# Gated delta-rule attention and routed experts: a new order of the turn, the key convolution in the queries' buffer, accumulator pairs assigned piece by piece

## The chip, the cores and the metric

The kernel runs on one core of a Trainium2 chip. The metric is the device time of one execution in microseconds (us). The engines of the core are TensorE (PE, with its weight loads as PEld), VectorE (DVE), ScalarE (ACT), GpSimd (POOL) and SyncE (SP), which only issues transfers. Each engine works off its own list of instructions in the order written; semaphores are the only tie between them. A difference of about 0.3% is the smallest that a measurement of this kernel can tell from none.

## What is computed

One transformer block on 4 sequences of 1024 positions with 256 channels. The part that matters here is the attention: 16 heads of width 64 with a gated delta rule, clipped.

```python
q = einsum('btd,cd->bct', h, Wq); k = ...Wk; v = ...Wv
q = silu(causal_conv(q)); k = silu(causal_conv(k)); v = silu(causal_conv(v))   # 4 taps
k = k / max(norm(k), 1e-12)
alpha = sigmoid(h @ Wa.T + ba); beta = sigmoid(h @ Wb.T + bb)
def step(S, (kt, vt, qt, at, bt)):
    v_old = S @ kt
    dS = outer(vt - at * v_old, kt)
    S = clip(at * S + bt * dS, -5, 5)
    return S, S @ qt
x = x + ga * (y * silu(h @ Wg.T + bg)) @ Wo.T
x = x + gb * moe(layernorm(x))          # 8 experts, 2 per token
```

## The kernel before, in words

The program is a chain of stages: `front` (layer norm, gates, step sizes), `delta_fast` (the whole attention recurrence), `judge`, `attn_out`, `moe`. The change is in `delta_fast` alone.

`delta_fast` works in 16 **turns** (`TURNS`), one for each pair of heads and pair of sequences. A turn does three things at once, each for another unit: `it` runs from -1 to 17; unit `u = it` is **prepared** (`prep`), unit `tc = it - 1` goes through its recurrence (`chain`), and unit `tb = it - 2` gets the bound that tells whether the clip could matter. A turn is cut into 16 slots `c`, one for each chunk of 64 positions of the chain; in each slot the chain does one link: `seed_u` and `state_into_u` (PE), `keep_u` (ACT), `state_sum` (PE), `state` (DVE, a copy for `c = 0`). Between the links stand pieces of the preparation, in an order written out by hand, `if prep and c == 5: ...`, on ACT, DVE and PE. On PE a slot has two places, ahead of `state_sum` and behind it.

The preparation of a unit, with the line of its work in brackets:

- K: `proj_k` (PE L976, 4 matrix products of 128x512 for each of the two sequences), `first_k` (ACT L530), `taps_k` (DVE L730, three passes for each sequence), `silu_k` (ACT L544).
- `kk` (PE L1012), 64x64 products of the keys with each other, two blocks `h`, each written in two halves of 32 rows in the trace.
- `decay(u, h)` (DVE L799), a scan over a row of step sizes that SP loads into the one buffer `d_al`; the load for `h = 1` waits until the scan for `h = 0` has read it. `solve_matrix(u, h)` (DVE L811, two passes), `join` (ACT L574), `turn_matrix` (DVE L819), `scalars` (DVE L828 to L834).
- `solve` (POOL L671 and L676): 31 rows of a forward substitution, in `d_TT`, two instructions each.
- meanwhile Q and V: `proj_qv(u, j, i)` for j = 0 to 3 (Q of two sequences, V of two), `first_qv`, `taps_qv`, `silu_qv`; `k_turned` (PE L1045) and `keep_k`; `kq` (PE L1012 with `d_qT`) and `attention` (DVE L857); `decayed_q` (DVE L851).
- when the solve is done: `turn_x` (DVE L872) and `rows_of_x` (DVE L879) transpose its result. `cross_first` (PE L1104) needs `rows_of_x` only; `keep_x` (ACT L588) and `cross_second` (PE L1117) need `turn_x` too, and `cross_second` needs `keep_cross_first` (ACT L595). `keep_cross` (ACT L602) ends that part. Then `v_turned` (PE L1045) and `scale_v` (DVE L866), `decayed_x` (DVE L883), `w_products` (PE L1139) and `keep_w` (ACT L616), `largest_k` (DVE L840), and K of unit u + 1, which begins the next turn.
- of the bound: `bound_terms` (POOL L687), `z_turned` (PE L1091), `bound_scan` (DVE L786), `bound_max` (DVE L793), `update_max` (DVE L768). Of the output: `y_of_state` (L1190), `y_of_u` (L1202), `turn_y` (DVE L760). POOL also decays the keys, `decay_k` (L703), which `state_sum` needs; it waits for `largest_k` and for `w_products`.

All pieces of the preparation that PE writes share four PSUM banks, as two **pairs** (`pair(at)`, banks 4 and 5, or 6 and 7). Before, a table gives each piece a place `AT_...` from 0 to 19 in a ring, and its pair is the place modulo 2. A piece may write a pair once the piece ahead of it on that pair has been read; these are the waits in `proj_k`, `proj_qv`, `kk`, `kq`, `turned` and so on. `conv_dst` says where a convolution is built: Q in `d_qT`, K in the memory of `d_TT` and `d_Tq` (`k_made`), V in that of `d_Xn`. As `d_TT` holds the solve and then the cross products, `first_k` waits for `s_x2` (`keep_cross`).

## Time and profile before

| | us |
|---|---|
| median of three runs | 2378.34 (2376.22 to 2382.27) |
| the profiled execution | 2367.01 |
| its span | 2365.4 |
| first and last `turn_matrix` (DVE L819), 15 turns apart | 105.6 and 1537.7 |
| PE, DVE, POOL, ACT busy | 81%, 63%, 42%, 32% of the span |

The profiled execution is 11.3 us shorter than the median, and 1.6 us of it lie around the span. In the profile a line like `L811 DVE TENSOR_TENSOR d_TT<-d_ps,d_D` is one instruction of VectorE written in line 811, with the tile that it writes ahead of the arrow. `[1.07 <-DMA d_al]` behind a row is the idle time of that engine just before it, and what ended it.

### The profile page before, as it was taken

What the parts mean: (1) busy time and instruction counts of PE and PEld (TensorE: products, weight loads), DVE (VectorE), ACT (ScalarE), POOL (GpSimd) and SP (SyncE); (2) the same over time, 40 slices, a digit from 0 to 9 for tenths busy, and PEclk for the clock granted to TensorE, in tenths of its full rate; (3) what the DMA queues carried; (4) which work ended last, traced back from release to release, by engine and by line L of the source; (5) the groups of instructions that cost most, each with busy time, mean ns of one, the idle gap of its engine ahead of it and who ended that gap; (6) DMA issues with size and microseconds to landing.
All of it is one profiled execution on the core that took longest, in us unless ns stands there. A gap on an engine that the chain in (4) does not pass through costs nothing. (4 is left out here: it accounts for less than half of the span.)

```text
span 2365.4 us, 59283 instructions
## 1 busy us (share of the span) xinstructions
PE 1924.9 (81%) x24750; PEld 1379.2 (58%) x24750; DVE 1489.1 (63%) x2181; ACT 760.4 (32%) x1250; POOL 1004.0 (42%) x1316
## 2 busy tenths in 40 slices
...
DMA packets 89029, 156.52 MB, mean 66 GB/s; under 512 B 15676, under 2 KB 54084, under 8 KB 87564
## 3 DMA queue, kind: packets, MB, share of 16 engines
...
## 5 line engine op out<-in xcount | busy, mean ns | idle before, releaser
L976 PE MATMUL d_ps<-hT,d_w 128*128 128x512 f32 x768 | 414.4, 659 | 16.3 <-DMA d_cw<-convp_in 11.9
L703 POOL TENSOR_TENSOR d_ktok<-d_ktok,decay_tok 128x512 f32<-128x512 f32 x64 | 95.6, 1523 | 510.0 <-DVE d_kmax L840 487.3
L676 POOL TENSOR_TENSOR d_TT<-d_TT,d_tmp 128x31 f32<-128x31 f32 (+15 forms) x496 | 284.0, 573 | 38.9
L671 POOL TENSOR_TENSOR d_tmp<-d_Tq,d_TT 128x31 f32<-128x31 f32 (+15 forms) x496 | 262.8, 530 | 73.8 <-DVE d_TT L834 36.2
L976 PEld LDWEIGHTS d_ps<-hT,d_w 128*128 128x128 f32 x768 | 138.4, 206 | 121.0 <-issue 89.7
L1157 PE MATMUL d_ps<-d_Vp,d_XTz 64*64 64x64 f32 x2048 | 143.2, 261 | 65.3 <-DVE d_S L750 64.3
L569 ACT ACTIVATE d_U<-d_ps 128x128 f32<-128x128 f32 x256 | 70.2, 274 | 383.1 <-PE d_ps L1165 379.8
L750 DVE SCALAR_TENSOR_TENSOR d_S<-d_S,gamma_chunk,d_ps 128x64 f32<-128x64 f32 x448 | 106.9, 291 | 135.2 <-PE d_ps L1174 135.1
L1157 PEld LDWEIGHTS d_ps<-d_Vp,d_XTz 64*64 64x64 f32 x2048 | 111.1, 163 | 125.0 <-issue 124.7
L2043 POOL DMA_INDIRECT out<-m_yo,m_slot_i x71 | 112.7, 1587 | 131.6 <-DVE m_yo L2143 86.2
L1784 POOL TENSOR_TENSOR y<-y,g_sb 128x512 f32<-128x512 f32 x64 | 102.5, 1632 | 124.2 <-ACT g_sb L1768 123.6
L2022 ACT ACTIVATE m_hm<-m_ps,m_b_tile 128x128 f32<-128x128 f32 x284 | 81.2, 368 | 226.8 <-PE m_ps L2191 226.8
L730 DVE SCALAR_TENSOR_TENSOR d_Xn<-d_ps,d_cw,d_Xn 128x1023 f32<-128x1023 f32 (+2 forms) x96 | 122.8, 1279 | 42.8 <-ACT d_Xn L530 41.6
L2181 PE MATMUL m_ps<-m_w,m_xs 128*128 x284 | 138.3, 610 | 8.3 <-issue 6.5
L1202 PE MATMUL d_ps<-d_U,d_A 64*64 64x64 f32 x2048 | 130.0, 249 | 6.9
L2202 PE MATMUL m_ps<-m_w,m_hm 128*128 x568 | 134.4, 380 | 0.0
L1202 PEld LDWEIGHTS d_ps<-d_U,d_A 64*64 64x64 f32 x2048 | 95.9, 151 | 61.9 <-issue 39.5
...
L1647 PE MATMUL o_pg<-h_split,wg_split 128*128 128x512 f32 x384 | 92.5, 399 | 39.3 <-DVE wo_split L1640 31.9
L730 DVE SCALAR_TENSOR_TENSOR d_qT<-d_ps,d_cw,d_qT 128x1023 f32<-128x1023 f32 (+2 forms) x96 | 121.3, 1277 | 1.2
L1012 PE MATMUL d_ps<-d_kT 64*64 64x64 f32 x2048 | 115.7, 280 | 6.8 <-ACT d_kT L544 6.8
L1647 PE MATMUL o_po<-wo_split,y_split 128*128 128x256 f32 x768 | 105.8, 305 | 16.2 <-DVE y_split L1640 16.2
...
## 6 DMA issues: line engine op xcount, KB each, us to landing
...
y_scratch<-d_yT SPq DMA_DIRECT2D x256, 64.0 KB, 2.0
d_arow<-ab_scratch SPq DMA_DIRECT2D x128, 128.0 KB, 3.0
...
```

The source lines that it names most:

```text
L671: nc.gpsimd.tensor_tensor(tv, Tq[:, s + 1:, s].rearrange("p (r a) -> p r a", a=1).broadcast_to([P, left, known]), X[:, s, 0:known].rearran ...
L676: nc.gpsimd.tensor_tensor(X[:, s + 1:, 0:known], X[:, s + 1:, 0:known], tv, ALU.subtract).then_inc(s_sub, 1)
L730: nc.vector.scalar_tensor_tensor(out=dst[:, j + 1:], in0=src[:, 0:T - 1 - j], scalar=cw[:, u // BP % 2, n, 2 - j:3 - j], in1=dst[:, j + 1: ...
L750: last = nc.vector.scalar_tensor_tensor(out=S[:, (c + 1) % SLOTS, b2, :], in0=S[:, c % SLOTS, b2, :], scalar=gC[:, b2, tc * NCW + c:tc * N ...
L976: return nc.tensor.matmul(dst[:, g, :], w[:, m % 2, n, dc, :], hT[:, dc, at:at + G], start=(dc == 0), stop=(dc == DC - 1))
L1012: last = nc.tensor.matmul(chunks(pair(at), CW)[rows64(b2), c, :], kT[rows64(h), c, b2, :], by(c, b2), start=True, stop=True)
L1157: last = nc.tensor.matmul(u_ps(c)[rows64(b2), h, :], XTz[rows64(b2), tc % 2, h * NCW + c, :], Vp[rows64(b2), c, rows64(h)], start=True, st ...
L1202: last = nc.tensor.matmul(y_ps(c, h, b2), A[rows64(b2), tc % 2, h, c, :], U[rows64(b2), c % KEPT, h, :].rearrange("p (j v) -> p j v", j=2) ...
L1647: ins = nc.tensor.matmul(dst, lhs(a).bitcast(F32R), rhs(b).bitcast(F32R), start=first and n == 0, stop=last and n == 2)
L2043: nc.gpsimd.indirect_dma_start(out, bass.IndirectOffsetOnAxis(ap=slot_i[:, j:j + 1], axis=0), yo[:, j % YRING, :], None, compute_op=ALU.ad ...
L2181: last = nc.tensor.matmul(ps[:, j % 2, :], xs[:, j % 2, dc * P:(dc + 1) * P], w1_s[:, bass.ds(e, 1), dc, :].rearrange("p a f -> p (a f)"), ...
L2202: last = nc.tensor.matmul(dst, hm[:, j % 2, f * P:(f + 1) * P], w2_s[:, bass.ds(e, 1), f, :].rearrange("p a d -> p (a d)"), start=f == 0, ...
```

## The change

The piece order of a turn is written anew on ACT, DVE and PE; POOL and SP are as before. K's convolution is built in `d_qT`, so `first_k` waits for `kq` and `decayed_q` of the unit ahead, no longer for `keep_cross`, and `first_qv` of Q waits for `silu_k`. The ring is gone; each piece has its pair, 0 or 1, by name, and each wait for a pair names the piece that is now ahead on it. Instructions and their sizes are the same. The core of the diff, one or two lines of each of the order tables:

```diff
-RING = 20
-(AT_KK0, AT_KK1, AT_Q0, AT_Q1, AT_KT0, AT_V0, AT_KT1, AT_KQ0, AT_V1, AT_Z0,
- AT_KQ1, AT_P, AT_Z1, AT_X, AT_VT0, AT_VT1, AT_K0, AT_K1, AT_WA, AT_WB) = range(RING)
+(AT_KK0, AT_Q0, AT_V0, AT_KT0, AT_Z0, AT_KQ1, AT_P, AT_X, AT_K0, AT_WA, AT_WB,) = (0,) * 11
+(AT_KK1, AT_Q1, AT_KQ0, AT_KT1, AT_V1, AT_Z1, AT_VT0, AT_VT1, AT_K1,) = (1,) * 9
...
-            return (qT[:, b2, :], k_made[b2], v_made)[n]
+            return (qT[:, b2, :], qT[:, b2, :], v_made)[n]
...
             def first_k(u, b2):
...
-                act.wait_ge(s_x2, u)
+                act.wait_ge(s_kq, 2 * u)
+                act.wait_ge(s_qg, u)
...
                 if i < 2:
-                    act.wait_ge(s_kq, 2 * u)
-                    act.wait_ge(s_qg, u)
+                    act.wait_ge(s_ksilu, 2 * u + 2)
...
                     if prep and c == 12:
                         taps_qv(u, 3, (2,))
+                        attention(u, 1)
+                        rows_of_x(u)
                         turn_x(u)
-                        rows_of_x(u)
-                    if prep and c == 13:
-                        attention(u, 1)
...
                     if b2 == 0:
                         if it >= 0:
-                            pe.wait_ge(s_V, 2 * it + 1)
+                            pe.wait_ge(s_x2, it + 1)
...
                     if h == 0:
                         if it >= 1:
-                            pe.wait_ge(s_wt, 2 * it - 1)
+                            pe.wait_ge(s_wt, 2 * it)
...
                     else:
-                        if it < TURNS - 1:
-                            pe.wait_ge(s_ktap, 6 * it + 12)
-                        else:
-                            pe.wait_ge(s_V, 2 * it + 2)
+                        pe.wait_ge(s_wt, 2 * it + 1)
```

The last piece is `w_products(u, 1)`: both W products stand on pair 0 now, so the second waits until `keep_w(u, 0)` has read the first, and `kk(u + 1, 0)` waits until `keep_w(u, 1)` has.

**Place 1, PE, the cross products (end of the solve).** L1104 (after: L1097) is `cross_first`, L1091 (L1087) `z_turned(1)`, L1157 and L1165 (L1147, L1155) the chain's `seed_u` and `state_into_u`, L1174 (L1164) `state_sum`, L1117 (L1110) `cross_second`, L1045 (L1041) `v_turned`. Before:

```order
L1104 MATMUL d_ps<-d_Xn,d_TTx 32x32 x64
L1091 MATMUL d_ps<-ident,d_Z 128x2x64 x8
L1157 MATMUL d_ps<-d_Vp,d_XTz 64x64 x4
L1165 MATMUL d_ps<-d_S,d_WT 64x64 x4
L1117 MATMUL d_ps<-d_Tq,d_TT 32x32 x32
L1174 MATMUL d_ps<-d_U,d_ktok 64x64 x4
L1117 MATMUL d_ps<-d_Tq,d_TT 32x32 x32
L1045 MATMUL d_ps<-ident,d_vT 128x128 x8
L1157 MATMUL d_ps<-d_Vp,d_XTz 64x64 x4
L1165 MATMUL d_ps<-d_S,d_WT 64x64 x4
L1045 MATMUL d_ps<-ident,d_vT 128x128 x4
```

After:

```order
L1087 MATMUL d_ps<-ident,d_Z 128x2x64 x8
L1097 MATMUL d_ps<-d_Xn,d_TTx 32x32 x32
L1147 MATMUL d_ps<-d_Vp,d_XTz 64x64 x4
L1155 MATMUL d_ps<-d_S,d_WT 64x64 x4
L1097 MATMUL d_ps<-d_Xn,d_TTx 32x32 x32
L1164 MATMUL d_ps<-d_U,d_ktok 64x64 x4
L1041 MATMUL d_ps<-ident,d_vT 128x128 x4
L1110 MATMUL d_ps<-d_Tq,d_TT 32x32 x64
L1041 MATMUL d_ps<-ident,d_vT 128x128 x4
L1147 MATMUL d_ps<-d_Vp,d_XTz 64x64 x4
L1155 MATMUL d_ps<-d_S,d_WT 64x64 x4
```

`z_turned(1)` stands ahead of `cross_first`, which is cut in two by a link of the chain, and half of the V transposes stand ahead of `cross_second`.

**Place 2, DVE, the key convolution of the next unit.** L730 (L729) are `taps_k`, L840 (L839) `largest_k`, L768 (L767) `update_max`, L748 (L747) the chain's first `state`. Before:

```order
L866 TENSOR_TENSOR d_Vp<-d_ps,d_n 128x1024
L730 SCALAR_TENSOR_TENSOR d_TT<-d_ps,d_cw,d_TT 128x1023
L730 SCALAR_TENSOR_TENSOR d_TT<-d_ps,d_cw,d_TT 128x1022
L730 SCALAR_TENSOR_TENSOR d_TT<-d_ps,d_cw,d_TT 128x1021
L730 SCALAR_TENSOR_TENSOR d_Tq<-d_ps,d_cw,d_Tq 128x1023
L730 SCALAR_TENSOR_TENSOR d_Tq<-d_ps,d_cw,d_Tq 128x1022
L730 SCALAR_TENSOR_TENSOR d_Tq<-d_ps,d_cw,d_Tq 128x1021
L840 TENSOR_REDUCE d_kmax<-d_ktok 128x128
L768 TENSOR_REDUCE d_um<-d_U 128x128
L748 COPY d_S<-d_ps 128x64 x2
L799 SCALAR_TENSOR_TENSOR d_D<-d_al,d_msk 128x1024
```

After:

```order
L865 TENSOR_TENSOR d_Vp<-d_ps,d_n 128x1024
L839 TENSOR_REDUCE d_kmax<-d_ktok 128x128
L729 SCALAR_TENSOR_TENSOR d_qT<-d_ps,d_cw,d_qT 128x1023
L729 SCALAR_TENSOR_TENSOR d_qT<-d_ps,d_cw,d_qT 128x1022
L729 SCALAR_TENSOR_TENSOR d_qT<-d_ps,d_cw,d_qT 128x1021
L729 SCALAR_TENSOR_TENSOR d_qT<-d_ps,d_cw,d_qT 128x1023
L729 SCALAR_TENSOR_TENSOR d_qT<-d_ps,d_cw,d_qT 128x1022
L729 SCALAR_TENSOR_TENSOR d_qT<-d_ps,d_cw,d_qT 128x1021
L747 COPY d_S<-d_ps 128x64 x2
```

`largest_k` is ahead of the taps and `update_max(2)` two slots earlier; the taps write `d_qT`.

**Place 3, PE and DVE, the start of the turn.** On PE, L1012 (L1008) is `kk`, L976 (L972) `proj_qv(0)`, L1190 and L1202 (L1180, L1192) the outputs. PE before:

```order
L1012 MATMUL d_ps<-d_kT 64x64 x16
L1174 MATMUL d_ps<-d_U,d_ktok 64x64 x4
L1190 MATMUL d_ps<-d_S,d_qg 64x2x32 x4
L1202 MATMUL d_ps<-d_U,d_A 64x2x32 x4
L1157 MATMUL d_ps<-d_Vp,d_XTz 64x64 x4
L1165 MATMUL d_ps<-d_S,d_WT 64x64 x4
L1012 MATMUL d_ps<-d_kT 64x64 x16
L1190 MATMUL d_ps<-d_S,d_qg 64x2x32 x4
L1174 MATMUL d_ps<-d_U,d_ktok 64x64 x4
L1202 MATMUL d_ps<-d_U,d_A 64x2x32 x4
L1012 MATMUL d_ps<-d_kT 64x64 x16
L1157 MATMUL d_ps<-d_Vp,d_XTz 64x64 x4
```

PE after:

```order
L1164 MATMUL d_ps<-d_U,d_ktok 64x64 x4
L1008 MATMUL d_ps<-d_kT 64x64 x16
L1180 MATMUL d_ps<-d_S,d_qg 64x2x32 x4
L1147 MATMUL d_ps<-d_Vp,d_XTz 64x64 x4
L1155 MATMUL d_ps<-d_S,d_WT 64x64 x4
L1008 MATMUL d_ps<-d_kT 64x64 x16
L1164 MATMUL d_ps<-d_U,d_ktok 64x64 x4
L1008 MATMUL d_ps<-d_kT 64x64 x16
L1147 MATMUL d_ps<-d_Vp,d_XTz 64x64 x4
L1155 MATMUL d_ps<-d_S,d_WT 64x64 x4
L1192 MATMUL d_ps<-d_U,d_A 64x2x32 x4
L1164 MATMUL d_ps<-d_U,d_ktok 64x64 x4
```

The first `state_sum` is ahead of `kk`, one `kk` block is left for the slot behind, and no projection is ahead of the third `state_sum` (the last row here); before, `proj_qv(0)` stands there, two rows below the piece shown. On DVE, L799 (L798) is `decay`, L811 (L810) `solve_matrix`, L760 (L759) `turn_y`, L750 (L749) `state`. DVE before:

```order
L799 SCALAR_TENSOR_TENSOR d_D<-d_al,d_msk 128x1024
L750 SCALAR_TENSOR_TENSOR d_S<-d_S,gamma_chunk,d_ps 128x64 x2
L811 TENSOR_TENSOR d_TT<-d_ps,d_D 128x512
L811 TENSOR_TENSOR d_TTx<-d_ps,d_D 128x512
L760 STREAM_TRANSPOSE d_yT<-d_ps 128x512 x2
L750 SCALAR_TENSOR_TENSOR d_S<-d_S,gamma_chunk,d_ps 128x64 x2
L799 SCALAR_TENSOR_TENSOR d_D<-d_al,d_msk 128x1024
L811 TENSOR_TENSOR d_TT<-d_ps,d_D 128x512
L811 TENSOR_TENSOR d_TTx<-d_ps,d_D 128x512
```

DVE after:

```order
L798 SCALAR_TENSOR_TENSOR d_D<-d_al,d_msk 128x1024
L767 TENSOR_REDUCE d_um<-d_U 128x128
L749 SCALAR_TENSOR_TENSOR d_S<-d_S,gamma_chunk,d_ps 128x64 x2
L810 TENSOR_TENSOR d_TT<-d_ps,d_D 128x512
L810 TENSOR_TENSOR d_TTx<-d_ps,d_D 128x512
L749 SCALAR_TENSOR_TENSOR d_S<-d_S,gamma_chunk,d_ps 128x64 x2
L759 STREAM_TRANSPOSE d_yT<-d_ps 128x512 x2
L798 SCALAR_TENSOR_TENSOR d_D<-d_al,d_msk 128x1024
L810 TENSOR_TENSOR d_TT<-d_ps,d_D 128x512
L810 TENSOR_TENSOR d_TTx<-d_ps,d_D 128x512
```

`turn_y` stands behind the third `state` (the second L749 here), just ahead of the second `decay`, and `update_max(3)` has gone from ahead of `turn_matrix` to behind the first `decay`.

## Rows read from the trace of the kernel before

**Rows 1.** The page: each engine's busy time, share of the span, instructions.
```profile
PE 1924.9 (81%) x24750; PEld 1379.2 (58%) x24750; DVE 1489.1 (63%) x2181; ACT 760.4 (32%) x1250; POOL 1004.0 (42%) x1316
```

**Rows 2.** One line of the kernel, `turn_matrix`: count, durations, first and last start.
```profile
L819 DVE STREAM_TRANSPOSE d_Tq<-d_TT x16: 1917/1956/1989, 105.6 to 1537.7; 128x1024 f32<-128x1024 f32 x16
```

**Rows 3.** DVE in order of time: start, duration, operation [idle before, releaser]; four stations.
```profile
815.82 1.93 DVE L872 STREAM_TRANSPOSE d_Tq<-d_TT 128x1024 f32<-128x1024 f32 x1 [5.73 <-POOL d_TT L676]
...
867.81 1.94 DVE L819 STREAM_TRANSPOSE d_Tq<-d_TT 128x1024 f32<-128x1024 f32 x1 [1.17 <-ACT d_TT L574]
...
911.86 1.95 DVE L872 STREAM_TRANSPOSE d_Tq<-d_TT 128x1024 f32<-128x1024 f32 x1 [3.27 <-POOL d_TT L676]
...
961.61 1.95 DVE L819 STREAM_TRANSPOSE d_Tq<-d_TT 128x1024 f32<-128x1024 f32 x1 [1.21 <-ACT d_TT L574]
```

**Rows 4.** POOL in order of time: end of one solve, start of the next.
```profile
911.78 1.92 POOL L687 TENSOR_TENSOR d_Z<-d_um,d_kmax 128x1024 f32<-128x1024 f32 x1
...
966.66 0.25 POOL L671 TENSOR_TENSOR d_tmp<-d_Tq,d_TT 128x31 f32<-128x31 f32 x1 [2.09 <-DVE d_TT L834]
```

**Rows 5.** Groups of instructions by line: busy, mean ns | idle before, releaser; `silu_k(1)`, `keep_w`.
```profile
L616 ACT ACTIVATE d_WT<-d_ps 128x1024 f32<-128x1024 f32 x32 | 32.8, 1024 | 21.8 <-PE d_ps L1139 21.8
...
L544 ACT ACTIVATE d_kT<-d_Tq 128x1024 f32<-128x1024 f32 x16 | 16.9, 1057 | 20.6 <-DVE d_Tq L730 20.6
```

**Rows 6.** PE in order of time, behind the solve that ended at 815.8.
```profile
819.76 3.49 PE L1104 MATMUL d_ps<-d_Xn,d_TTx 32*32 32x32 f32 x123
823.18 1.97 PE L1091 MATMUL d_ps<-ident,d_Z 128*128 128x128 f32 x8
...
826.28 1.92 PE L1117 MATMUL d_ps<-d_Tq,d_TT 32*32 32x32 f32 x64
```

**Rows 7.** ACT in order of time, the same turn: `keep_cross`, `first_k`.
```profile
830.51 2.04 ACT L602 ACTIVATE d_XTz<-d_ps 32x1024 f32<-32x1024 f32 x2 [3.81 <-PE d_ps L1117]
838.82 1.20 ACT L530 ACTIVATE d_TT<-d_ps,d_cw 128x1024 f32<-128x1024 f32 x1 [6.27 <-PE d_ps L976]
```

**Rows 8.** DVE in order of time, the same turn, from `scale_v` to `solve_matrix`.
```profile
837.12 1.23 DVE L866 TENSOR_TENSOR d_Vp<-d_ps,d_n 128x1024 f32<-128x1024 f32 x1 [1.14 <-PE d_ps L1045]
840.06 3.92 DVE L730 SCALAR_TENSOR_TENSOR d_TT<-d_ps,d_cw,d_TT 128x1023 f32<-128x1023 f32 x3 [1.71 <-ACT d_TT L530]
843.89 3.91 DVE L730 SCALAR_TENSOR_TENSOR d_Tq<-d_ps,d_cw,d_Tq 128x1023 f32<-128x1023 f32 x3
847.71 2.28 DVE L840 TENSOR_REDUCE d_kmax<-d_ktok 128x128 f32<-128x2048 f32 x1
...
852.01 2.28 DVE L799 TENSOR_TENSOR_SCAN d_D<-d_al,d_msk 128x1024 f32<-128x1024 f32 x1
...
861.96 2.28 DVE L799 TENSOR_TENSOR_SCAN d_D<-d_al,d_msk 128x1024 f32<-128x1024 f32 x1
...
864.94 0.68 DVE L811 TENSOR_TENSOR d_TTx<-d_ps,d_D 128x512 f32<-128x512 f32 x1
```

**Rows 9.** PE in order of time, the same turn's start: `kk`, `proj_qv`.
```profile
849.52 1.91 PE L1012 MATMUL d_ps<-d_kT 64*64 64x64 f32 x30
...
859.00 2.07 PE L976 MATMUL d_ps<-hT,d_w 128*128 128x512 f32 x2
```

**Rows 10.** Stretches: us, busy by engine (PE, PEld, DVE, ACT, POOL), granted clock, DMA share, GB/s.
```profile
848.70:862.20 13.50, 13.30 (x243) 11.04 (x236) 7.96 (x14) 2.05 (x5) 7.97 (x5) 0.50 0.46 118
...
931.00:944.00 13.00, 10.15 (x138) 5.53 (x140) 10.26 (x9) 5.00 (x6) 0.00 (x0) 1.00 0.01 1
944.30:947.60 3.30, 3.30 (x99) 3.30 (x91) 2.10 (x2) 1.71 (x3) 1.71 (x2) 0.50 0.03 7
947.70:962.00 14.30, 12.96 (x269) 8.87 (x265) 11.57 (x18) 3.22 (x6) 6.16 (x4) 1.00 0.62 155
```

**Rows 11.** DVE in order of time, the next turn: last tap of K, second `decay`.
```profile
939.71 3.91 DVE L730 SCALAR_TENSOR_TENSOR d_Tq<-d_ps,d_cw,d_Tq 128x1023 f32<-128x1023 f32 x3
...
955.75 2.29 DVE L799 TENSOR_TENSOR_SCAN d_D<-d_al,d_msk 128x1024 f32<-128x1024 f32 x1 [1.07 <-DMA d_al<-steps_scratch]
```

264 lines of the change are left out of this document (130 added, 134 removed).

## The prediction

> **What bounds the kernel now.** The page comes first, and it misleads: PE is busy for 81% of the span [rows 1], so one looks for fewer or faster products. The view of single lines corrects this. `turn_matrix` runs once a turn, and 15 turns lie between its first start at 105.6 and its last at 1537.7 [rows 2]: 1432.1 / 15 = 95.47 us a turn. What decides those 95.47 us is a ring, read off DVE in order of time [rows 3]. From `turn_matrix` at 867.81 to `turn_x` at 911.86 are 44.05 us, and DVE stood idle for 3.27 us ahead of `turn_x` (5.73 in the turn ahead), each time for POOL. This is the **solve half**: POOL starts at 966.66, 5.05 after `turn_matrix` at 961.61, and is done at 911.78, right when `turn_x` starts [rows 3, 4]. PE's load there costs nothing as long as DVE is ready before POOL.
>
> The other part, from `turn_x` to the next `turn_matrix`, is the **K half**: the cross products, the convolution of the next keys, `kk`, `solve_matrix`, `join`. It took 51.99 us from 815.82 to 867.81 and 49.75 from 911.86 to 961.61 [rows 3]. The mean is 95.47 - 44.05 = 51.42, so about (51.99 - 51.42) / (51.99 - 49.75) = one turn in four is of the short kind. What parts the two kinds is TensorE's clock at the start of the turn [rows 10]: granted 0.50 (1.2 GHz) for all of 848.7 to 862.2 in the long one; in the short one 0.50 only from 944.3 to 947.6, then 1.00 (2.4 GHz). Both falls follow a time in which PE waits for K's taps (PE is busy for 10.15 of the 13.0 us ahead of 944.3). In the short turn W products and `kk` then filled the stretch without a gap (3.30 busy of 3.30), and the clock rose; in the long one it rose only after a large product, `proj_qv`, had run at 859.00 [rows 9].
>
> **The change, part by part.** Nothing is added or removed, so every term is a move. Times below are counted from `turn_x`'s place x = 815.82 in the long turn.
>
> (1) *Solve half.* `attention(1)` (1.2 us) comes ahead of the transposes and has to fit into DVE's idle time of 3.27 to 5.73 us [rows 3]. The V convolution of the first sequence starts earlier. `turn_y` moves within the half. POOL's list is unchanged. Price: 0, hidden behind POOL; if the cover failed, each us of lateness of DVE would be 15 us in all.
>
> (2) *Cross products.* Before, `cross_first` ends at 819.76 + 3.49 = x+7.4, `cross_second` starts at 826.28 and `keep_cross` ends at 830.51 + 2.04 = x+16.7 [rows 6, 7]. After, `rows_of_x` comes first, which would free `cross_first` 2 us earlier. But on PE `z_turned(1)` is now ahead of it, and waits for POOL's `bound_terms` of 1.92, which starts when the solve ends [rows 4]. So: 1.9, `z_turned` 1.9 to x+3.8 [rows 6], half of `cross_first` 1.8, a link of the chain 1.2 (from the end of `z_turned` at 825.15 to 826.28 it took 1.13), the other half 1.8: x+8.6. `keep_cross_first`, which I price like `keep_cross` at 2.04, x+10.7. `cross_second` as one piece 2 x 1.92 = 3.84 [rows 6], x+14.5. `keep_cross` x+16.6. Net -0.1: the 2 us are spent on the transposes of Z.
>
> (3) *Taps of K.* The K projection needs `keep_cross` (pair 0), x+16.6. Half of the V transposes lie behind it, interleaved with the projections. A 128x512 product takes 2.07 at the low clock [rows 9], about half at the high one. With the clock rising as now around x+19 the second V transposes are out at x+20.7, `scale_v(1)` 1.23 and `largest_k` 2.28 [rows 8] follow: x+24.2. `first_k` is done at x+23.8, so `largest_k` is what the taps wait for. They start at x+24.2, before at 840.06, also x+24.2. They end at T = x+32.0 as before. Net 0; bounds -0.4 (the short turn's start) and +1.4 (the clock rises one K product later, at the low price).
>
> (4) *From the taps to the first `decay`.* Before: 843.89 + 3.91 = T = 847.80 to 852.01, 4.2 us, with `largest_k` 2.28 in it [rows 8]. After, the path runs over ACT: `silu_k(1)` 1.06, `keep_w(1)` 1.02 [rows 5], then `keep_u(0)`, `state_sum` and `state`, for which I take 1.2, what a link of the chain took in (2): the first `decay` at T+3.3. The new wait is here: with both W products on pair 0, `kk(0)` and `keep_u(0)` are queued behind `keep_w(1)`, and `kk` starts at T+2.9, where it started at about T+1.6 (849.52 is its third row [rows 9]). I get a gain of 0.9 on DVE and a loss of 1.3 on PE.
>
> (5) *From there to the end of `solve_matrix`.* Before, at the low clock: 864.94 + 0.68 = T+17.8 [rows 8]. After, at the low clock: `kk` blocks of 1.8 each, at T+2.9, T+6.2 and T+8.2, links of 1.0 to 1.5 between them, the third `state` at T+12.2 because neither a projection of 2.07 nor a fourth `kk` block stands ahead of it. `turn_y` 1.3, then the second `decay` from T+13.8 to T+16.1. The last `kk` block stands behind `proj_qv(0)` and a link, to about T+16.2; two passes of 0.68 give T+17.5. Net -0.3. At the high clock I get T+14.5. Before, with T = 939.71 + 3.91 = 943.62, the second `decay` at 955.75 waits for its transfer [rows 11]; 2.29 of its own and 1.4 for the two passes (864.24 to 865.62 in the long turn [rows 8]) give T+15.8. Net -1.3.
>
> *Sum.* A long turn: 51.99 - 0.3 = 51.69. A short one: 49.75 - 1.3 + 0.2 for (4)'s later start = 48.65. The sum hangs on how many turns are short. PE now stands still three times ahead of `kk`: from the end of the K projections to the end of the first taps, about 2 us, as the outputs that filled this time have moved two slots ahead; between the two W products, 1 us for `keep_w(0)`; and 2.3 us from the last W product to `state_sum(0)`. The short turn's clock rose out of W products and `kk` without a gap; that sequence no longer occurs. I take no short turns: 51.69 - 51.42 = +0.27 a turn, 15 x 0.27 = **+4 us**. Against the profiled execution 2367.0 + 4 = 2371; the median of the runs is 11.3 above it and I keep that distance: 2378.3 + 4 = **2382**.
>
> The Trainium skill, page "TensorE: Matmul & The Clock Gate", section "Why this matters for your kernels", says that gaps of idle time between bursts of products bring the clock back down, and that TensorE is to be kept busy. The trace agrees on the fall at 944.3 [rows 10]; on the long turn's stretch, busy for 13.30 of 13.50 us at 0.50, busy time alone did not bring it back. By the page's rule a `kk` stretch that is busy throughout would regain the clock soon, and every turn would be short.
>
> **Rivals.** *The clock comes back early.* The mechanism is the one of the short turn: `kk`, the links and the outputs now run with three blocks close together, and if that is enough the turns take 48.65: 15 x (48.65 - 51.42) = -42, 2337. If only today's share of one in four stays short: 0.25 x 48.65 + 0.75 x 51.69 = 50.93, 15 x -0.49 = -7, 2371. For it: 3.30 of 3.30 busy raised the clock once [rows 10]. Against it: 13.30 of 13.50 did not.
>
> *Slower: the clock rises later behind the cross products.* Half of the V transposes, 128 wide, now stand far ahead of the K projection, so the stretch that raised the clock is thinner. If the first two K products and the last V transposes run at 1.2 GHz, `largest_k` and the taps start 0.8 to 1.4 us later. With the +0.27 this is 15 x 1.1 to 15 x 1.7 = +16 to +25: 2394 to 2403. It decides against the kernel from a delay of 0.2 us a turn on, since 15 x 0.47 is 7.
>
> *The moves do not do what they say* in the solve half: DVE is late for the transposes, as `bound_max(0)` now holds `kq(1)`, which `attention(1)` waits for. The 3.27 to 5.73 us of idle time less 1.2 leave 2.1 to 4.5, so this needs a large error; 1 us of lateness gives +15, 2397.
>
> **How the numbers follow.** The forecast case, no short turns and the terms right to within 0.45 us a turn, has 0.42; all of it lies within 0.3% (7.1 us, about what a measurement of this kernel can tell from no change). The early clock, in whole or for a share of the turns, has 0.27, from 2337 to 2371. The late clock has 0.26, a late DVE 0.05: together 0.31 on the slow side. The range leaves out the last part of the early clock (0.1) and the end of the late one (0.1): 2350 to 2398; the forecast case alone is 2375 to 2386.
>
> **What would show it.** Right: the solve half stays 44.05; DVE's idle ahead of `rows_of_x` is several us and for POOL; `cross_first` starts 3.8 to 3.9 behind `rows_of_x`, as now; the taps of K start at x+24 right behind `largest_k`; the first `decay` starts 3.3 behind the end of the taps; the K half is 51.4 to 52.0 in nearly every turn; the granted clock is 0.50 across `kk` in all turns. Wrong: K halves of 49 or less in many turns (the early clock); taps later than x+24.8 (the late clock); a `rows_of_x` that follows `attention(1)` without idle time (DVE late).

## The result and the profile after

| | before | after |
|---|---|---|
| median of 8 runs beside each other, us | 2377.08 (2366.23 to 2382.27) | 2361.80 (2358.32 to 2365.61) |
| ratio, 95% interval | | 0.9946 [0.9931, 0.9961] |
| once more, beside each other, median | 2373.69 of 29 runs | 2365.27 of 10 runs, 0.9966 [0.9951, 0.9981] |
| the profiled execution, and its span | 2367.01, 2365.4 | 2365.61, 2364.0 |

By the two ratios the change makes the kernel faster by 0.3% to 0.5%. I forecast 2382, a little slower and no measurable difference. The time lies in my range, but the direction and the likeliest case were wrong.

The two profiled executions differ by only 1.4 us and mislead: before's lay low among its runs, after's high. I therefore profiled both kernels a second time (`before_again`, `after_again`). The page and one line of the kernel, `turn_matrix`, which answer to [rows 1, 2]:

```profile
PE 1902.9 (80%) x24750; PEld 1356.3 (57%) x24750; DVE 1499.0 (63%) x2181; ACT 756.1 (32%) x1250; POOL 980.7 (41%) x1316
```

```profile
L818 DVE STREAM_TRANSPOSE d_Tq<-d_TT x16: 1925/1946/1960, 105.1 to 1535.3; 128x1024 f32<-128x1024 f32 x16
```

15 turns take 1430.2 us (before: 1432.1), in the second execution 1424.7 (before: 1435.6).

**A long turn of after.** DVE in order of time, from the first transpose at x = 1006.05 to the next `turn_matrix` (start, duration, operation; it answers to [rows 3, 8]):

```profile
1006.05 2.05 DVE L878 STREAM_TRANSPOSE d_Xn<-d_TT 128x1024 f32<-128x1024 f32 x1 [6.64 <-POOL d_TT L675]
...
1028.43 2.28 DVE L839 TENSOR_REDUCE d_kmax<-d_ktok 128x128 f32<-128x2048 f32 x1
1030.62 7.73 DVE L729 SCALAR_TENSOR_TENSOR d_qT<-d_ps,d_cw,d_qT 128x1023 f32<-128x1023 f32 x6
...
1041.65 3.81 DVE L798 TENSOR_TENSOR_SCAN d_D<-d_al,d_msk 128x1024 f32<-128x1024 f32 x1
...
1051.27 2.25 DVE L798 TENSOR_TENSOR_SCAN d_D<-d_al,d_msk 128x1024 f32<-128x1024 f32 x1
...
1054.60 0.68 DVE L810 TENSOR_TENSOR d_TTx<-d_ps,d_D 128x512 f32<-128x512 f32 x1
...
1057.46 1.95 DVE L818 STREAM_TRANSPOSE d_Tq<-d_TT 128x1024 f32<-128x1024 f32 x1 [1.80 <-ACT d_TT L572]
```

The solve half is as before, bounded by POOL with 6.64 us of idle time on DVE. The K half is 51.41: taps at x+24.6, first `decay` at x+35.6, 3.3 behind the end of the taps, end of `solve_matrix` at x+49.2. From 910.47 on the turns repeat to within 0.06 us (95.54 to 95.60). PE and ACT behind the same x (they answer to [rows 6, 7]):

```profile
1007.95 1.97 PE L1087 MATMUL d_ps<-ident,d_Z 128*128 128x128 f32 x8 [8.02 <-POOL d_Z L686]
1009.85 1.92 PE L1097 MATMUL d_ps<-d_Xn,d_TTx 32*32 32x32 f32 x64
...
1012.89 1.92 PE L1097 MATMUL d_ps<-d_Xn,d_TTx 32*32 32x32 f32 x64
...
1017.04 3.63 PE L1110 MATMUL d_ps<-d_Tq,d_TT 32*32 32x32 f32 x128 [0.77 <-ACT d_TT L593]
```

```profile
1020.71 2.04 ACT L600 ACTIVATE d_XTz<-d_ps 32x1024 f32<-32x1024 f32 x2 [3.81 <-PE d_ps L1110]
```

`rows_of_x` is out of the way 2 us earlier, and `z_turned(1)` (L1087) spends it: `keep_cross` (L600) starts at x+14.7 as before. The clock, in stretches from x+35.5 to x+48.0 of five turns (columns as in [rows 10], the granted clock is the third number from the end):

```profile
375.30:387.80 12.50, 12.02 (x249) 8.10 (x244) 10.21 (x17) 2.42 (x5) 4.12 (x2) 1.00 0.64 150
...
661.60:674.10 12.50, 12.00 (x257) 8.21 (x251) 10.36 (x17) 2.20 (x5) 4.34 (x2) 1.00 0.62 155
754.50:767.00 12.50, 12.31 (x214) 10.00 (x212) 10.21 (x13) 0.83 (x3) 2.04 (x2) 0.52 0.43 113
...
1041.50:1054.00 12.50, 12.31 (x215) 9.94 (x211) 10.08 (x14) 0.83 (x3) 1.81 (x1) 0.53 0.44 112
1137.10:1149.60 12.50, 12.31 (x214) 9.94 (x210) 10.09 (x14) 0.83 (x3) 1.79 (x1) 0.53 0.44 115
```

In the turns of 339.79 and 626.11 the clock stays at 2.4 GHz and their K halves are 48.56 and 48.76; in the other turns from the fourth on the stretch is at 0.50 to 0.54, nearly all of it 1.2 GHz, and the K halves are 51.4 to 52.2. The first two turns are neither kind (49.63 and 50.16) and are taken up below.

**Where the time went.** From the DVE rows of all 15 turns of both executions of each kernel, K halves in us:

| | before | after |
|---|---|---|
| turns 4 to 15: mean | 51.37 | 51.35 |
| of these under 50.3 (short) | 8 of 24, mean 49.77 | 2 of 24, mean 48.87 |
| the others (long) | 52.17 | 51.57 |
| turns 1 to 3: mean (lowest, highest) | 51.15 (48.08, 52.79) | 48.86 (47.38, 50.16) |
| solve half, mean of all turns | 44.26 | 44.32 |
| last `turn_matrix` to the first cast of the next stage | 152.6, 152.4 | 149.5, 149.3 |

The steady turns gained nothing. The first three gained 3 x (51.15 - 48.86) = 6.9 us, the drain behind the last turn 3.1, and 0.8 went back in the solve halves (15 x 0.05): about -9.5 (-0.3, -6.9, +0.8, -3.1), against -8.1 and -12.8 by the two ratios. The -6.9 is a mean of two executions that lie apart: the first three K halves sum to 152.0 and 154.9 in before, to 148.3 and 144.8 in after. Two kernels from below, which measured like before and like after, agree with it: 153.8 in `before_max_ahead`, 148.0 in `after_k_in_tt`. From the cast on, the stages behind run the same instructions, but took 675.1 and 682.5 in the two executions of before and 679.2 and 682.0 in those of after: the first page of before owes 7 us to that.

### The profile page after: what moved, and what is told of

It reads as the page before. It is cut to its first block and busy times, and to the rows that moved or that the text cites. A ratio compares the mean times of both kernels' runs of the same rounds, so it can differ in the third digit from the quotient of the medians.

```text
span 2364.0 us, 59315 instructions
## 1 busy us (share of the span) xinstructions
PE 1902.9 (80%) x24750; PEld 1356.3 (57%) x24750; DVE 1499.0 (63%) x2181; ACT 756.1 (32%) x1250; POOL 980.7 (41%) x1316
## 3 DMA queue, kind: packets, MB, share of 16 engines
q1 hardware_dynamic: 72860, 124.76, 17.5%
## 5 line engine op out<-in xcount | busy, mean ns | idle before, releaser
L972 PE MATMUL d_ps<-hT,d_w 128*128 128x512 f32 x768 | 429.0, 676 | 28.1 <-DVE d_qT L729 12.8
L670 POOL TENSOR_TENSOR d_tmp<-d_Tq,d_TT 128x31 f32<-128x31 f32 (+15 forms) x496 | 279.1, 563 | 75.2 <-DVE d_TT L833 37.6
L675 POOL TENSOR_TENSOR d_TT<-d_TT,d_tmp 128x31 f32<-128x31 f32 (+15 forms) x496 | 269.5, 543 | 38.9
L702 POOL TENSOR_TENSOR d_ktok<-d_ktok,decay_tok 128x512 f32<-128x512 f32 x64 | 66.5, 1060 | 463.8 <-PE d_ps L1129 442.9
L729 DVE SCALAR_TENSOR_TENSOR d_qT<-d_ps,d_cw,d_qT 128x1023 f32<-128x1023 f32 (+2 forms) x192 | 242.8, 1277 | 21.1 <-ACT d_qT L528 17.7
L972 PEld LDWEIGHTS d_ps<-hT,d_w 128*128 128x128 f32 x768 | 139.1, 209 | 125.3 <-issue 81.2
L749 DVE SCALAR_TENSOR_TENSOR d_S<-d_S,gamma_chunk,d_ps 128x64 f32<-128x64 f32 x448 | 109.3, 302 | 88.1 <-PE d_ps L1164 84.0
L1147 PEld LDWEIGHTS d_ps<-d_Vp,d_XTz 64*64 64x64 f32 x2048 | 113.4, 163 | 85.6 <-issue 84.3
L1147 PE MATMUL d_ps<-d_Vp,d_XTz 64*64 64x64 f32 x2048 | 145.5, 261 | 16.7 <-DVE d_S L749 14.4
L729 DVE SCALAR_TENSOR_TENSOR d_Xn<-d_ps,d_cw,d_Xn 128x1023 f32<-128x1023 f32 (+2 forms) x96 | 122.2, 1273 | 43.7 <-ACT d_Xn L528 42.5
L1087 PE MATMUL d_ps<-ident,d_Z 128*128 128x128 f32 x256 | 50.7, 363 | 113.9 <-POOL d_Z L686 113.9
L1192 PE MATMUL d_ps<-d_U,d_A 64*64 64x64 f32 x2048 | 132.7, 249 | 7.8
L528 ACT ACTIVATE d_qT<-d_ps,d_cw 128x1024 f32<-128x1024 f32 x64 | 77.1, 1205 | 175.6 <-issue 96.9
L694 POOL MEMSET d_TT<- 128x1024 f32 x16 | 15.2, 952 | 283.3 <-DVE d_Tq L818 283.3
L1192 PEld LDWEIGHTS d_ps<-d_U,d_A 64*64 64x64 f32 x2048 | 100.4, 152 | 50.7 <-issue 25.0
```

The costliest lines, as they stand in the source:

```text
L670: nc.gpsimd.tensor_tensor(tv, Tq[:, s + 1:, s].rearrange("p (r a) -> p r a", a=1).broadcast_to([P, left, known]), X[:, s, 0:known].rearran ...
L675: nc.gpsimd.tensor_tensor(X[:, s + 1:, 0:known], X[:, s + 1:, 0:known], tv, ALU.subtract).then_inc(s_sub, 1)
L729: nc.vector.scalar_tensor_tensor(out=dst[:, j + 1:], in0=src[:, 0:T - 1 - j], scalar=cw[:, u // BP % 2, n, 2 - j:3 - j], in1=dst[:, j + 1: ...
L749: last = nc.vector.scalar_tensor_tensor(out=S[:, (c + 1) % SLOTS, b2, :], in0=S[:, c % SLOTS, b2, :], scalar=gC[:, b2, tc * NCW + c:tc * N ...
L972: return nc.tensor.matmul(dst[:, g, :], w[:, m % 2, n, dc, :], hT[:, dc, at:at + G], start=(dc == 0), stop=(dc == DC - 1))
L1147: last = nc.tensor.matmul(u_ps(c)[rows64(b2), h, :], XTz[rows64(b2), tc % 2, h * NCW + c, :], Vp[rows64(b2), c, rows64(h)], start=True, st ...
```

## The experiments

Fifteen-turn times below run from the first start of `turn_matrix` to the last, in one profiled execution; before is 1432.1 and 1435.6, after 1430.2 and 1424.7.

### The same two kernels again, and the transposes swapped alone

`before_again` is before, `after_again` is after, unchanged.

> The kernel before, unchanged, to see how far one execution of it differs from the next. Theory 'mix': its executions differ in how many of the 15 K halves (from turn_x or rows_of_x to the next turn_matrix) are short (under 50.5 us, clock back at 2.4 GHz within the kk stretch) or long (52 us); the profiled one of the prediction held more short ones than is usual, so this one has a sum of 15 turns (first to last start of turn_matrix) above 1432, up to 1441, and a span that follows it. Rival 'elsewhere': the 15 turns take 1432 again within 2 us, and what differs between executions lies in the stages behind the recurrence. Ratio to before 1.000.

> The changed kernel, unchanged, beside before on one chip. Theory 'mix': ratio about 0.994 to 0.996; in the profile most K halves are 51.4 us, the sum of 15 turns is 1425 to 1432, so the distance to the sum of before_again is 5 to 12 us. Rival 'elsewhere': the sums of 15 turns of the two differ by under 3 us, and the last unit's recurrence and what follows it carry the rest.

Ratios 1.0006 [0.9992, 1.0019] and 0.9966 [0.9951, 0.9981]. The gain is there again, a little smaller; two executions of one kernel differ by up to 5.5 us in the fifteen turns. Both of my cases for before hold in part: its two spans differ by 11.8 us, of which 3.6 lie in the turns and 7.4 in the stages behind.

`before_rows_first` makes one of the change's moves in before:

```diff
                     if prep and c == 12:
                         taps_qv(u, 3, (2,))
-                        turn_x(u)
                         rows_of_x(u)
+                        turn_x(u)
```

> The kernel before with rows_of_x ahead of turn_x on VectorE, nothing else. cross_first needs rows_of_x only. Theory 'the ring is bound link by link': cross_first starts 2.05 behind the first transpose in place of 3.8, cross_second at 8.7 in place of 10.5, and each K half is 1.7 shorter: 15 x 1.7 = 25 us, ratio 0.989. Rival 'the K half is held elsewhere' (by the V transposes, bound_max or the K projection): under 8 us, ratio 0.997 or more.

2366.31, ratio 0.9948 [0.9921, 0.9975], fifteen turns 1428.5. `cross_first` starts at x+2.10 instead of x+3.83, `keep_cross` ends at x+15.0 instead of x+16.7, the taps start at x+22.9 in the mean instead of x+24.1, and the K half is 50.52 in the mean, 0.8 less than before's 51.33. Solve halves of 45.3 in several turns give some of it back. The time lies between my two cases, at half of the 25 us. This one swap is worth as much as the whole change, though its twelve runs spread widely: four lie from 2342.5 to 2354.3, eight from 2363.8 to 2372.9, and the profiled one (2367.15) is of the eight. Its first three K halves sum to 146.8: the swap alone takes as much from them as the change does. In before the head of the K half can be shortened, and in the steady turns the change spends that on `z_turned(1)`.

### After, with the cross products in before's order

```diff
                     if prep and c == 13:
                         cross_first(u, 0)
+                        cross_first(u, 1)
+                    if tb >= 0 and c == 13:
+                        z_turned(it, 1)
                     if prep and c == 14:
-                        v_turned(u, 0, 0)
-                        cross_second(u, 0)
                         cross_second(u, 1)
+                        v_turned(u, 0, 0)
                         v_turned(u, 0, 1)
```

(`z_turned(1)` is taken from ahead of `cross_first`, `cross_second(0)` stands where `cross_first(1)` was, and `keep_cross_first` goes one slot ahead on ACT.)

> The changed kernel with the cross products in the order of before on TensorE (cross_first whole, then z_turned(1), cross_second in two halves, V transposes behind them) and keep_cross_first right behind keep_x on ScalarE; rows_of_x stays ahead of turn_x. Theory 'z_turned(1) ahead of cross_first spends what rows_of_x first would give': cross_first starts at 2.05 in place of 3.8, cross_second at 8.7 in place of 11.0, the K half is 1.5 to 2 us shorter than in after: ratio to before 0.983 to 0.986. Rival: the taps start when they do now, at 24.6, as scale_v(1) and largest_k hold them: ratio 0.994.

2341.01 (2334.33 to 2346.43), ratio 0.9868 [0.9846, 0.9891], close to the 0.983 to 0.986 of my theory: 1.3% in place of the change's 0.3% to 0.5%, faster than both kernels. DVE and PE of one turn, x = 1086.09:

```profile
1086.09 2.05 DVE L878 STREAM_TRANSPOSE d_Xn<-d_TT 128x1024 f32<-128x1024 f32 x1 [6.44 <-POOL d_TT L675]
...
1107.79 2.27 DVE L839 TENSOR_REDUCE d_kmax<-d_ktok 128x128 f32<-128x2048 f32 x1
```

```profile
1088.19 3.63 PE L1097 MATMUL d_ps<-d_Xn,d_TTx 32*32 32x32 f32 x128 [8.02 <-DVE d_Xn L878]
1091.75 1.97 PE L1087 MATMUL d_ps<-ident,d_Z 128*128 128x128 f32 x8
1094.85 1.92 PE L1110 MATMUL d_ps<-d_Tq,d_TT 32*32 32x32 f32 x64
1097.12 1.92 PE L1110 MATMUL d_ps<-d_Tq,d_TT 32*32 32x32 f32 x64
```

`cross_first` starts at x+2.1, and `z_turned(1)` falls into the time in which PE waits for ACT's copy. From the third turn on `keep_cross` ends at x+15.0 and the taps start at x+22.5 to x+24.0; K halves are 47.7 to 50.9, fifteen turns 1407.8. The order of the change in this place costs about 20 us (1427.5, the mean of after, less 1407.8; by the medians 2365.27 less 2341.01, 24 us). The run moves three things together: `z_turned(1)`, the cut of `cross_first` by a link, and `keep_cross_first` on ACT. What each is worth by itself was not measured.

### Single parts of the change taken back

`after_wb_pair1`: the second W product on pair 1, as in before, with the waits that belong to it.

```diff
-(... AT_K0, AT_WA, AT_WB,) = (0,) * 11
-(... AT_VT1, AT_K1,) = (1,) * 9
+(... AT_K0, AT_WA,) = (0,) * 10
+(... AT_VT1, AT_K1, AT_WB,) = (1,) * 10
...
-                        pe.wait_ge(s_wt, 2 * it + 1)
+                        if it < TURNS - 1:
+                            pe.wait_ge(s_ktap, 6 * it + 12)
```

> The changed kernel with the second W product on pair 1 in place of pair 0, so that it waits for the last tap of K as before, kk(0) only for the first keep_w and kk(1) for the second. Theory 'the pair of W': the W product moves behind the taps, keep_w(1) and the chain's keep_u(0) behind it follow 1.0 to 1.5 us later, the first decay starts at T+4.5 in place of T+3.3 (T is the end of K's taps), and the K half grows by 1: +15 us, ratio near 1.001. Rival 'W and kk without a gap bring the clock back early': more K halves under 50.5, the K half no longer, ratio 0.990 to 0.996.

2381.65, ratio 1.0037 [1.0022, 1.0051], fifteen turns 1442.8. They grow by 15 us as in my theory; the ratio is above its 1.001. The first `decay` starts 4.7 behind the end of the taps (T) in the mean, with pair 0 it was 3.2. On pair 1 the product waits for the last tap of K; on pair 0 it only waits for a copy on ACT. The pair is worth about 15 us of the fifteen turns.

`after_k_in_tt`: K's convolution in the memory of `d_TT` and `d_Tq`, with before's waits.

```diff
-            return (qT[:, b2, :], qT[:, b2, :], v_made)[n]
+            return (qT[:, b2, :], k_made[b2], v_made)[n]
```

> The changed kernel with K's convolution built in the memory of TT and Tq as before, with the waits of before for it (first_k on keep_cross, Q's first_qv on kq and decayed_q). Both theories: no change, since the K projection, on pair 0, waits for keep_cross in any case; ratio 0.994 to 0.997, all stations of the K half within 0.1 us. If the queries' memory matters the taps start later than 24.6 and the kernel is over 5 us slower than after.

2366.09, ratio 0.9962 [0.9948, 0.9977], as after: the memory of the convolution has no effect.

`after_largest_behind`: `largest_k` behind the taps, as before.

```diff
                         scale_v(u, 1)
-                        largest_k(u)
...
                         taps_k(u + 1, 1, (2,))
+                    if prep and c == 15:
+                        largest_k(u)
```

> The changed kernel with largest_k behind the taps of K, as before. The taps may then start when first_k is done, 0.4 us earlier at most (24.2). Theory 'largest_k holds the chain': GpSimd's decay_k waits for largest_k, 2.28 behind the taps, and takes 1 to 1.5 us, state_sum(0) waits for it, so the first decay moves from T+3.3 to about T+4.5; net +0.8 a turn, +12 us, ratio near 1.000. Rival 'it is hidden': ScalarE's two silu and keep steps of 3.3 us cover it, the turn gains 0.4, ratio 0.991 to 0.994.

2362.02 (2348.16 to 2371.78), ratio 0.9946 [0.9925, 0.9968], as after; neither of my cases (near 1.000, or 0.991 to 0.994) came. The profiled execution is the slowest of its eight, with fifteen turns of 1435.8. In it the taps start 0.4 earlier in the mean and the first `decay` comes at T+4.1 instead of T+3.2, so at that point it is 0.5 behind. The times show no such loss; what makes up for it was not found.

`after_qv_ahead`: the first projection of Q ahead of the third `state_sum`, as before.

```diff
+                    if prep and c == 2:
+                        proj_qv(u, 0, 0)
                     if prep and c == 3:
                         kk(u, 1, 1)
```

(It goes from behind `state_sum(2)` to ahead of it.)

> The changed kernel with one product put back: proj_qv(0,0) stands ahead of the third state_sum on TensorE, as before. Theory 'start of the turn': where the kk stretch runs at 1.2 GHz this product takes 2.07 us ahead of state_sum(2), which the third state and with it the second decay and solve_matrix wait for, so the long K half grows from 51.5 by 1 to 2 us and the kernel by 10 to 25 us (ratio to before 1.000 to 1.006). Rival 'the gain lies in the cross products or at the taps': no change, ratio 0.994 to 0.997.

2371.34, ratio 0.9985 [0.9973, 0.9998]. Long K halves grow to 52.7 to 53.4, the second `decay` comes at x+47.0 instead of x+45.2, as the third `state` waits for the projection. In this profile every second turn is short, so that its fifteen turns (1429.8) are hardly longer than after's. Why they are short there is not known. The move of this projection is a gain of some 0.2% to 0.4%.

`before_max_ahead`: `update_max(3)` in slot 0 in before, to test one explanation of the shorter drain.

```diff
+                    if tb >= 0 and c == 0:
+                        update_max(tb, 3)
...
-                    if tb >= 0 and c == 2:
-                        update_max(tb, 3)
```

> Before, with update_max(3) on DVE moved from slot 2 to slot 0, as the change does: the one move held responsible for 2.6 us of the 3.1 us by which the drain behind the last turn became shorter. Theory: from the last turn_matrix to the first cast of the next stage 150.0 instead of 152.6; the turns get no shorter (it now stands between decay and solve_matrix, in idle time): ratio 0.998 to 1.000. Rival: the drain is shortened by the new order as a whole and not by this move: 152.5, ratio 1.000; or the move delays solve_matrix by its own length each turn, ratio over 1.002.

2376.75, ratio 1.0001 [0.9992, 1.0011], the drain is 152.5: my explanation fell. PE at the end of the chain in this kernel, and in after:

```profile
1664.76 0.49 PE L1165 MATMUL d_ps<-d_S,d_WT 64*64 64x64 f32 x8
...
1671.04 1.97 PE L1091 MATMUL d_ps<-ident,d_Z 128*128 128x128 f32 x8
```

```profile
1657.05 0.49 PE L1155 MATMUL d_ps<-d_S,d_WT 64*64 64x64 f32 x8
...
1661.17 1.97 PE L1087 MATMUL d_ps<-ident,d_Z 128*128 128x128 f32 x8
```

From the last link's product to the transposes of Z behind the outputs are 6.28 us in before and in this kernel, 4.12 in after: the outputs of five chunks stand between them there, of three here. These 2.2 us are most of the 3.1. It is read from the traces; no run took it away alone.

### Does TensorE's clock part long from short turns?

`after_filler`, `cross_filler` and `before_filler` add matrix products of 128x320 that nobody reads, into PE's idle time in the K half (the expectations of after and before call them 128x128; they were 320 columns wide). In after:

```diff
+            def filler(tc, n):
+                ...
+                for _ in range(n):
+                    nc.tensor.matmul(ps[:, 0, 3 * DH:], ident[:], hT[:, 0, 0:G - 3 * DH], start=True, stop=True)
...
                     if prep and c == 15:
+                        filler(tc, 5)
                         w_products(u, 0, 0)
                         w_products(u, 0, 1)
+                        filler(tc, 2)
                         w_products(u, 1, 0)
...
+                        filler(tc, 3)
```

> After, with idle time of PE in the K half filled by matrix products 128x128 whose result nobody reads (it adds work and leaves nothing out): 5 ahead of the first W product (PE waits for the first taps of K there), 2 between the two W products, 3 behind the last W product. Theory: what parts long from short turns is TensorE's clock while kk runs; with large products in the gaps it is 1.00 there in nearly all turns, the K half is 47.4 to 50.2 in nearly all (51.4 in 11 of 15 now), the next solve half 45.4 to 45.8 instead of 44.1; per turn 0.6 to 1.5 less, 9 to 22 us in all: ratio to before 0.985 to 0.991. Rival: the clock of kk is a companion and not the cause, or the products don't hold it up; then they are mere work on PE's list, K halves stay at 51.4 or get longer by up to 1: ratio 0.995 to 1.001.

> The kernel after with the cross products in the order of before (2341.0), with the same added products as in the kernel above. Its K halves were 47.7 to 50.85 without them. Theory (clock of kk decides): where its turns already run kk at the high clock there is nothing left to win there; I expect K halves of 47.7 to 49 and a ratio of 0.984 to 0.988. Rival (added products are only work): K halves longer by 0.5 to 1, ratio 0.990 to 0.993.

> Before, with 4 products 128x128 that nobody reads between the two W products, where PE waits for the second taps of K. Theory: kk runs at 1.00, the K half is 49.6 to 50.0 in nearly all turns (short kind of before) instead of one in three to four: 15 x 1.5 = 22 us at most, ratio 0.990 to 0.994. Rival: no effect of the clock: ratio 1.000 to 1.004.

After with them: 2372.20, ratio 0.9985 [0.9975, 0.9995]; the fast kernel of the section above: 2349.99, 0.9885 [0.9867, 0.9903]; before: 2379.01, 1.0008 [0.9989, 1.0027]. After, the added products and the clock behind x = 815.00, and DVE:

```profile
843.27 2.96 PE L1140 MATMUL d_ps<-hT,ident 128*128 128x320 f32 x10 [1.51 <-ACT d_U L567]
...
850.01 1.88 PE L1140 MATMUL d_ps<-hT,ident 128*128 128x320 f32 x6
```

```profile
850.50:863.00 12.50, 11.65 (x260) 8.56 (x258) 8.92 (x13) 1.53 (x5) 3.40 (x3) 1.00 0.41 113
```

```profile
853.43 2.61 DVE L798 TENSOR_TENSOR_SCAN d_D<-d_al,d_msk 128x1024 f32<-128x1024 f32 x1
...
863.81 0.68 DVE L810 TENSOR_TENSOR d_TTx<-d_ps,d_D 128x512 f32<-128x512 f32 x1
```

The clock is held at 1.00, and from the first `decay` to the end of `solve_matrix` are 11.1 us instead of 13.6. But 6.2 us of added work, of which 2.96 could only start when ACT had read the same bank, moved the first `decay` from x+35.6 to x+38.4. In the sum nothing is gained: after loses 0.2% to 0.4% by it, and the fast kernel's ratio lies between my two cases. In before the added products let nine K halves be short instead of four or five. In the turn of 816.10 they held the clock some four us longer, then it fell all the same (0.68 in 853.00:854.00, 0.50 behind that); five of the six K halves that stayed long rose to 53.3 to 53.7.

`after_lean_filler` and `cross_lean_filler` add less (5 and 2 products of 128x192 and 2 of 128x128), in a bank that ACT does not read then:

```diff
                     if prep and c == 15:
+                        filler(5, 5)
                         w_products(u, 0, 0)
                         w_products(u, 0, 1)
+                        filler(2, 5)
                         w_products(u, 1, 0)
...
+                        filler(2, 6)
```

> After, with smaller added products that nobody reads, sized to fit into PE's idle time: 5 of 128x192 ahead of the first W product, 2 between the W products, 2 of 128x128 behind the outputs that end the turn; they write a part of PSUM that ACT does not read at that time, so that they need not wait for keep_u(15). In the kernel with 128x320 products the granted clock was 1.00 all through kk and the first decay came to the end of solve_matrix in 10.9 us instead of 13.6, but the added products themselves ended late and moved the first decay from T+3.3 to T+5.65. Theory (the clock of kk parts long turns from short ones): first decay at T+2.7 to T+3.5, solve_matrix 10.9 later, K halves of 48.4 to 49.2 in nearly all turns, given back 1.5 in the next solve half; 15 x about 1 less than after: ratio to before 0.987 to 0.991. Rival (the gain was an artefact of the later start, the work before kk having piled up): K halves stay at 51.4, ratio 0.994 to 0.997.

> The kernel after with the cross products of before, and the same smaller added products. In its run without them the K halves were 47.7 to 50.85, so some turns lost the clock in kk. Theory: all turns at the high clock, K halves 47 to 48.5, ratio 0.981 to 0.986 (without: 0.9868). Rival: nothing gained, 0.986 to 0.990.

After: 2360.83, ratio 0.9940 [0.9922, 0.9959], fifteen turns 1418.6 in an execution that is the fastest of its six. The fast kernel: 2335.34 (2327.82 to 2338.95), ratio 0.9817 [0.9783, 0.9852], fifteen turns 1396.9. Four turns of after with the lean products, from x+35.5 to x+48.0; their K halves are, in this order, 50.8, 49.2, 50.6 and 49.2:

```profile
466.70:479.20 12.50, 10.73 (x204) 8.20 (x201) 10.34 (x13) 0.83 (x3) 1.52 (x1) 0.69 0.54 131
562.40:574.90 12.50, 11.14 (x210) 7.51 (x207) 10.84 (x15) 1.84 (x4) 0.92 (x1) 0.86 0.59 148
...
1037.10:1049.60 12.50, 10.70 (x196) 7.95 (x192) 10.34 (x13) 0.83 (x3) 1.28 (x1) 0.68 0.53 141
...
1323.70:1336.20 12.50, 11.28 (x209) 7.53 (x205) 10.70 (x15) 1.78 (x4) 0.75 (x1) 0.86 0.55 148
```

And the fast kernel with them, K halves 50.00, 47.24, 48.12 and 47.56:

```profile
460.90:473.40 12.50, 10.72 (x177) 7.65 (x174) 10.62 (x15) 1.04 (x4) 0.80 (x1) 0.67 0.59 149
555.90:568.40 12.50, 10.44 (x187) 6.47 (x176) 9.62 (x16) 3.39 (x6) 0.00 (x0) 1.00 0.69 182
647.50:660.00 12.50, 10.50 (x193) 6.68 (x188) 9.67 (x15) 2.56 (x4) 0.00 (x0) 1.00 0.67 168
739.80:752.30 12.50, 10.34 (x188) 6.45 (x185) 9.39 (x16) 3.09 (x6) 0.00 (x0) 1.00 0.75 182
```

The end of the K half follows the clock: from the first `decay` to the end of `solve_matrix` are 13.6 us at 0.53 (after), 13.2 at 0.69 and 11.7 at 0.86 (the first two turns above). The first `decay` starts at T+3.0 to T+3.1 in them, no later than in after, so the rival of a gain by a later start falls. Adding work that nobody needs shortens the K half: the mean of turns 4 to 15 of after falls from 51.35 to 50.24. From the third turn on the stretches of after stood at 0.64 to 0.86, and in the fast kernel only some were at 1.00, so my size of it (all turns at 48.4 to 49.2) was too large. On the times the lean products in after can't be told from none (0.9940 and 0.9946, 0.9966); in the fast kernel the ratio falls from 0.9868 to 0.9817, with intervals that overlap a little, from five and four runs. The best version is `cross_lean_filler`, 1.8% faster than before. What holds the clock in one turn and not in the next stays open.

## Why the prediction was wrong, point by point

- **The solve half and (1): right.** 44.05 taken, 44.0 to 44.2 measured in most turns; DVE waits 6.64 us for POOL. Some are longer because POOL starts later: in after five are 44.7 to 45.8, with POOL's first row 5.6 to 6.7 behind `turn_matrix` instead of 5.05, and each stands directly ahead of a short K half (45.79 ahead of 48.76, for one). A short turn is thus worth less than its K half says. Why the two go together I did not follow up. In before, too, the mean is 44.23 and not 44.05, so my 51.42 for its mean K half should have been 51.24, and 5 of its 15 K halves were short, not one in four.
- **(2), right.** Forecast x+8.6, x+14.5, x+16.6 for the ends of `cross_first`, `cross_second`, `keep_cross`; measured x+8.8, x+14.6, x+16.7. The run with before's order showed that the 2 us could have been kept, worth 20 us.
- **(3), right within 0.4.** Forecast x+24.2, measured x+24.6, for `scale_v(1)` came at x+21.2 and not at x+20.7. The rival of a late clock (x+24.8 or later) did not come in the steady long turns.
- **(4), right.** Forecast T+3.3, measured T+3.3. The pair is what makes it: T+4.7 without.
- **(5), within 0.6.** Forecast T+17.5, measured 1055.28 - 1038.35 = T+16.9: the second `decay` came at T+12.9, not T+13.8. Long turns 51.57 against 51.69.
- **No short turns: nearly right for steady turns.** 2 of 24 were short, 8 of 24 before. The mean was to go from 51.42 to 51.69 and went from 51.37 to 51.35: the loss of short turns and the shorter long ones cancel. The price of +0.27 was thus 0.3 too high, 3.5 us in twelve turns.
- **The step that failed is "I take no short turns: ... 15 x 0.27".** I multiplied the price of a steady turn without short ones by all fifteen. The first three are of another kind, and gave -6.9 where I had +0.8. Turn 1 (48.08 and 52.79 before, 49.63 and 49.10 after): there are no transposes of Z yet, so nothing stands between `rows_of_x` and `cross_first`, which starts at x+2.07 (151.28 for x = 149.21), not at x+3.80, and the taps start at x+22.9 and x+22.1, against x+24.4 in `before_again` (before's own first turn had the high clock and x+22.1). Turns 2 and 3 give -2.9 each, and there the K half's head is no shorter: in turn 2 `cross_first` starts early too, but a link cuts it in two, and the taps start at x+24.1 and x+23.7 as in before; in turn 3 everything is as in a steady turn. What differs beside the moves of a steady turn is the granted clock from x+35.5 to x+48.0: 0.72 and 1.00 in turn 2 of after (before: 0.53 and 0.57), 1.00 and 1.00 in turn 3 (before: 0.56 and 0.98). So short turns did come, at the start of the loop, and most of the -6.9 came with them. This is read from the traces, and turn 2 is not settled: in `after_k_in_tt` it takes 50.08 with the clock at 0.50 and taps from x+22.6. Why the clock is high just there is open.

```profile
151.28 3.62 PE L1097 MATMUL d_ps<-d_Xn,d_TTx 32*32 32x32 f32 x128 [16.20 <-DVE d_Xn L878]
...
341.70 1.97 PE L1087 MATMUL d_ps<-ident,d_Z 128*128 128x128 f32 x8 [7.87 <-POOL d_Z L686]
343.60 1.92 PE L1097 MATMUL d_ps<-d_Xn,d_TTx 32*32 32x32 f32 x64
```

Turn 2 of after, of after's second execution, and of before, columns as above:

```profile
279.70:292.20 12.50, 10.60 (x186) 7.50 (x180) 10.75 (x14) 0.83 (x3) 1.27 (x1) 0.72 0.51 142
...
280.40:292.90 12.50, 11.46 (x224) 7.62 (x224) 9.55 (x16) 3.55 (x7) 2.95 (x1) 1.00 0.65 173
...
277.20:289.70 12.50, 12.24 (x210) 9.85 (x208) 7.74 (x12) 0.56 (x2) 6.67 (x4) 0.53 0.54 127
```

- **A term was missing:** the drain behind the last turn, -3.1. I priced the turns and not what the new order leaves over at the end. The forecast's +4 and the -9.5 found are 13.5 apart: 7.7 from the first three turns, 3.5 from the steady ones, 3.1 from the drain, and -0.8 from the solve halves.
- **"I keep that distance" was a guess.** Before's median beside after was 2377.08 and 2373.69, not 2378.34; and the distance of a profiled execution to the median is luck: 11.3 then, -3.8 for after's.
- **The early clock** had 0.27 in my chances. As worked out (all turns short, or one in four) it did not come; it came in turns 2 and 3, which is a part of the gain. That the clock sets the end of the K half is shown by the runs with added products. The Trainium skill, page "TensorE: Matmul & The Clock Gate", section "Why this matters for your kernels", says to keep TensorE busy. The runs agree in that added 128x320 products in the gaps kept the granted clock at 1.00. They do not agree in that after's stretch of 1041.50, busy for 12.31 of 12.50 us, stayed at 0.53.

Terms of -0.3, -6.9, +0.8 and -3.1 make -9.5, the second ratio says -8.1, and the first says -12.8 with an interval of -9 to -16. The means of the turns come from two executions each, and the spread between two executions of one kernel is 3.5 to 5.5 us; what the rest is stays open.
